# Layer 1 attention of a two-layer network: other tiles, other masks, another order of the same sums

## The reference

```python
Q, K, V = x @ wq, x @ wk, x @ wv                  # 16 heads of 8
# a token sees, in its own block of 32 and the one ahead of it, the 32 last keys
base = (j > i) & (j <= i + W)
blk0 = (jnp.arange(nb) > 0)[:, None, None] | (j >= W)[None, :, :]
sc = jnp.einsum('bhnid,bhnjd->bhnij', Qb, Kw) / np.sqrt(D)
p = jax.nn.softmax(jnp.where(mask, sc, -jnp.inf)); local = p @ Vw
# 64 latents, each the mean of 8 tokens; token s sees latents up to s // 8
GQ = x @ wgq; GK = pool(x @ wgk); GV = pool(x @ wgv)
lmask = jnp.arange(N_LATENTS)[None, :] <= (jnp.arange(Sx) // chunk)[:, None]
rem = softmax(where(lmask, GQ GK^T / sqrt(8), -inf)) @ GV @ r_out_w
gl = sigmoid(einsum('bhsd,hd->bhs', Q, gate_local_w)); gr = sigmoid(... gate_remote_w)
out = (gl * local + gr * rem) @ w_out
```

## Time and profile before

| | us |
|---|---|
| median of 3 runs | 823.16 (821.97 to 823.99) |
| the profiled execution | 828.99 |
| its span, first to last instruction | 826.9 |
| mean granted TensorE clock, share of 2.4 GHz | 0.904 |
| layer 1 attention, from its first matmul to the end of its last addition | 259.6 to 618.6 |

### The profile page before, as it was taken

One profiled execution on the slowest core, in us unless ns is written; L12 is line 12 of the kernel. 1 busy time (PEld: TensorE's weight loads), 2 busy tenths in 40 slices (PEclk: granted clock), 3 DMA queues, 4 the chain that ended last, 5 costly groups with the idle time before them and its releaser, 6 DMA issues.

```text
span 826.9 us, 15605 instructions
## 1 busy us (share of the span) xinstructions
PE 654.0 (79%) x4213; PEld 542.3 (66%) x4217; DVE 448.2 (54%) x1243; ACT 375.0 (45%) x874; POOL 245.3 (30%) x292
## 2 busy tenths in 40 slices
PE   3859457763174799999999999999978899998950
PEld 3837346763073677777777787878757788887850
DVE  7488637751667867676776776676731111111116
ACT  2217414441023364646555555555314555555534
POOL 6065716656002222222222220000001343433430
PEclk9999669995555999999999999999967999999985
DMA  9992133341230000000000000000004444444539
GB/s 242 256 186 56 45 103 116 110 125 49 76 128 0 21 20 21 19 22 17 20 21 21 18 20 1 1 1 1 1 4 146 164 158 154 164 154 152 168 104 276
DMA packets 80840, 69.46 MB, mean 84 GB/s; under 512 B 8436, under 2 KB 66419, under 8 KB 80782
## 3 DMA queue, kind: packets, MB, share of 16 engines
q1 hardware_dynamic: 71616, 54.97, 23.9%
q0 software_dynamic: 6624, 12.70, 4.8%
q10 hardware_dynamic: 2542, 1.08, 0.5%
HBM read 22.63 MB, written 23.22 MB: 55 GB/s over the span
## 4 chain that ended last, share of the span: by engine, by line
PE 40%; issue 19%; SPq 19%; DVE 11%; DMA 6%; POOL 3%; ACT 1%; DVEq 1%; POOLq 0%; ACTq 0%; another core or an unknown queue 0%
PE psum L1424 9%; PE psum L1386 5%; PE psum L1405 5%; SPq L1097 5%; PE psum L1395 4%; SPq L1110 4%; PE psum L1432 3%; SPq L1120 3%; SPq L242 3%; DMA ydram<-arena,g_id 3%; PE psum L1371 3%; POOL ydram L819 2%; DMA arena<-ydram 2%; PE psum L1359 2%; PE psum L1380 2%
## 5 line engine op out<-in xcount | busy, mean ns | idle before, releaser
L678 POOL DMA_INDIRECT sorted<-xr_all,slot x96 | 94.7, 987 | 190.2 <-DVE arena L1654 162.7
L1209 POOL DMA_INDIRECT ydram<-arena,f_id x71 | 68.7, 967 | 241.4 <-DVE f_id L1185 220.5
L1550 ACT ACTIVATE arena<-arena 128x512 f32<-128x512 f32 x96 | 60.5, 630 | 133.9 <-DVE arena L1654 133.8
L1170 ACT ACTIVATE arena<-psum,b1T 128x128 f32<-128x128 f32 x284 | 81.2, 369 | 78.8 <-PE psum L1139 68.8
L1651 DVE TENSOR_REDUCE arena<-psum 128x8 f32<-128x512 f32 x96 | 66.4, 691 | 66.8 <-PE psum L1386 34.8
L1193 DVE TENSOR_TENSOR arena<-psum,b_bc 128x128 f32<-128x128 f32 x71 | 20.7, 292 | 145.5 <-PE psum L1150 74.8
L1424 PE MATMUL psum<-arena 128*128 128x66 f32 (+1 forms) x768 | 97.6, 267 | 0.1
L1424 PEld LDWEIGHTS psum<-arena 128*128 128x128 f32 x768 | 95.7, 196 | 0.3 <-ACTq L1556 0.3
L1139 PE MATMUL psum<-arena 128*128 128x128 f32 x568 | 82.4, 290 | 16.3 <-DMA arena<-arena 12.7
L1139 PEld LDWEIGHTS psum<-arena 128*128 128x128 f32 x568 | 71.3, 197 | 28.6 <-issue 21.6
L1150 PE MATMUL psum<-w,arena 128*128 x568 | 80.6, 285 | 0.4
(11 more groups left out here) (267 smaller groups left out, 1086.9 us busy)
## 6 DMA issues: line engine op xcount, KB each, us to landing
arena<-arena SPq DMA_DIRECT2D x71, 256.0 KB
arena<-ydram SPq DMA_DIRECT2D x24, 256.0 KB, 4.0
arena<-mix SPq DMA_DIRECT2D x40, 128.0 KB
sorted<-pre_row SPq DMA_DIRECT2D x1, 4680.0 KB
arena<-sorted SPq DMA_DIRECT2D x71, 65.0 KB
sorted<-pre_row SPq DMA_DIRECT2D x1, 2600.0 KB, 21.6
arena<-sorted SPq DMA_DIRECT2D x10, 260.0 KB, 3.1
x_all<-in_L_attn_x_dram SPq DMA_DIRECT2D x8, 256.0 KB, 5.4
```

The costliest lines, as they stand in the source:

```text
L678: g.indirect_dma_start(out=dst, out_offset=bass.IndirectOffsetOnAxis(ap=slot[:, choice, t:t + 1], axis=0), in_=xr_all[:, t, :], in_offset= ...
L1170: ins = act.activation(f_hT[rr % 4][:, j * P:(j + 1) * P], psum[:, 2 + rr % 2, j * P:(j + 1) * P], ACT.Relu, bias=b1T[:, bass.ds(e * FC + ...
L1209: g.indirect_dma_start(out=ydram, out_offset=bass.IndirectOffsetOnAxis(ap=f_id[rr][:, :], axis=0), in_=f_y[rr], in_offset=None, bounds_che ...
L1550: act.activation(c_p[s % 3], c_sx[s % 2], ACT.Exp).then_inc(c_pr, 1)
```

## The change

The whole attention of layer 1 is written anew; what it computes is the same.

- The window scores lie with 128 tokens on the partitions. Each block of 32 tokens and each group of 4 heads is a matmul of its own, of a 32x32 part of the array (32 channels of the group, 32 tokens) against 256 columns (4 heads x 64 key places); 64 of them a batch in place of 16, and no bf16 mask matmuls but four of 128 columns for the first block. Keys are masked by the head (`head_m`) and kept once per head; the queries are plain.
- Since a token sees exactly 32 of its 64 key places, DVE lays the two blocks over each other (`copy_predicated` by `later`), and maximum, subtraction, exponential and transposes work on 4 x 4 x 32 places. After the transposes `split` multiplies by `m_prev` and `m_cur` into two parts.
- `values` is, for each tile of 128 tokens, 32 matmuls of 32 weight columns against 36 columns (4 heads x 8 channels and the denominator), 128 a batch; `pick` and the mask by group go. The values and the gates are projected with tokens as the weights: 64 matmuls of 32 against 32 columns, and 16 for both gates.
- Latent scores, exponentials, transposes and products of tile t cover only the first 16 (t + 1) latents.
- The sum of window and latents is formed with tokens on the partitions, and transposed once (`cbT`).
- Four PSUM banks hold window scores of 256 tokens at a time, and all else passes a ring of the four others in the order of the lists `even` and `odd`.
- PE waits, before its first projection, for the routing to have read PSUM (`s_rt`), and the zeroing by GpSimd (`attn1_init`) moves to before the norm of layer 1. The scatters wait for a third as many softmaxes.
- Set-up: other masks, and tables padded with zeros; one more small load.

```diff
+            def scores(u):
+                b, s = u // 2, u % 2
...
+                emptied(pe, "Q", b)
+                emptied(pe, "K", b)
+                if u:
+                    pe.wait_ge(c_sxr, 2 * u)
+                for tt in range(2):
+                    for k in range(G):
+                        n = (2 * s + tt) * G + k
+                        for g in range(G):
+                            row = slice(W * g, W * g + W)
+                            mm = pe.matmul(psum[W * k:W * k + W, g, tt * 256:(tt + 1) * 256],
+                                           c_q[b % 2][row, n * W:(n + 1) * W], c_kz[b % 2][row, :, n * W:n * W + W2],
+                                           start=True, stop=(n > 0), skip_group_check=True)
...
+            def values(b, s):
...
+                    for g in range(G):
+                        for c, part in enumerate((c_pp, c_pc)):
+                            for k in range(G):
+                                n = t * G + k
+                                at_ = tt * G * HE + g * HE
+                                pe.matmul(o[W * k:W * k + W, at_:at_ + HE],
+                                          part[t % 2][:, g * P + k * W:g * P + (k + 1) * W],
+                                          c_v[b % 2][:, n + c, g, :, :].rearrange("p h e -> p (h e)"),
+                                          start=(c == 0), stop=(c == 1), skip_group_check=True)
...
+                if name == "V":
+                    for n in range(NB):
+                        for h in range(G):
+                            mm = pe.matmul(o[W * h:W * h + W, n * W:(n + 1) * W], xnT(b, n * W, (n + 1) * W),
+                                           wv_h[:, h, :, :], start=True, stop=True, skip_group_check=True)
...
+            for b in range(B):
+                latent_scores(b, 0)
+                latent_scores(b, 1)
+                transposes(b, 0)
+                transposes(b, 1)
+                remote("remT", b - 1)
+                scores(2 * b + 1)
+                latent_transposes(b, 0)
+                latent_transposes(b, 1)
+                remote("remo", b - 1)
+                values(b, 0)
+                project("Q", b + 1)
+                project("K", b + 1)
+                latent_scores(b, 2)
+                latent_scores(b, 3)
+                transposes(b, 2)
+                transposes(b, 3)
+                scores(2 * b + 2)
+                remote("cbT", b - 1)
...
+            def window_softmax(u):
...
+                    ch.link(v.copy_predicated(cur, later[:, :].bitcast(I32).unsqueeze(1).unsqueeze(1)
+                                              .to_broadcast([P, G, G, W]), sv[:, :, :, 0, :]))
+                    mx = c_mx.rearrange("p (g h) -> p g h", g=G)
+                    ch.link(v.tensor_reduce(mx, cur, AX, ALU.max))
...
+            def split(b, t):
+                o, free = filled(v, f"T{t}", b)
+                ov = o.rearrange("p (g q) -> p g q", g=G)
+                for part, m in ((c_pp, m_prev), (c_pc, m_cur)):
...
             pe.wait_ge(c_init, 1)
-            attn1(pe, attn1_pe)
+            pe.wait_ge(s_l1, 1)
+            pe.wait_ge(s_rt, 6)
+            attn1_pe(pe)
```

More of the change, by code:

```diff
@@ L1263, in build @@
[L1263 to L1273 removed]
+        c_p = [view(512) for _ in range(2)]
@@ new lines, in build, with ring_uses @@
+        c_q = [mix0[:, k * S:(k + 1) * S] for k in range(2)]
+        c_xp8 = cmp_[:, 0:NL * LH]
+        c_cb, c_cbT = mix0[:, 2 * S:3 * S], mix0[:, 3 * S:4 * S]
+        wv_h = wv1[:, :].rearrange("p (g h e) -> p h g e", g=G, h=G)
+        first = ["Q", "K", "V", "G", "GX", "GQ"]
+        even = ["L0", "L1", "T0", "T1", "-remT", "LT0", "LT1", "-remo", "O0", "+Q", "+K"]
+        odd = ["L2", "L3", "T2", "T3", "-cbT", "LT2", "LT3", "O1", "-out", "+V", "+G", "+GX", "+GQ"]
+        def ring_uses():
+            seq = [(n, 0) for n in first]
@@ new lines, in ring_uses, with slot_of @@
+            seq += [(n, B - 1) for n in ("remT", "remo", "cbT", "out")]
+            return {use: k for k, use in enumerate(seq)}
+        uses_of = ring_uses()
+        r_rdy = [sem(f"r_rdy{n}") for n in range(4)]
+        r_free = [sem(f"r_free{n}") for n in range(4)]
+        (c_init, c_xpr, c_sr, c_sxr, c_pr, c_lpr, c_cbr) = (
+            sem(n) for n in "c_init c_xpr c_sr c_sxr c_pr c_lpr c_cbr".split())
+        def slot_of(name, b):
+            k = uses_of[name, b]
+            return psum[:, 4 + k % 4, :], r_rdy[k % 4], r_free[k % 4], k // 4 + 1
@@ L1427, in local_out @@
-            def local_out(hf):
-                pe.wait_ge(c_zr, batch(cur) * 8 + (4 * hf + 4))
-                o, rdy = begin(acc(f"loc{hf}", cur))
-                for j in range(HB):
-                    mm = pe.matmul(o[:, order[j] * W:(order[j] + 1) * W], c_z[hf][:, j, :, :].rearrange("p g c -> p (g c)"),
-                                   pick[:, :], start=True, stop=True)
-                mm.then_inc(rdy, 1)
-            def tail(name):
-                if not prev:
+                b, s = u // 2, u % 2
@@ new lines, in scores, with transposes, latent_scores @@
+                mm.then_inc(c_sr, 1)
+            def transposes(b, t):
+                pe.wait_ge(c_pr, b * T + t + 1)
+                o, rdy = begin(f"T{t}", b)
+                for g in range(G):
+                    mm = pe.transpose(o[:, g * P:(g + 1) * P], c_p[t % 2][:, g * P:(g + 1) * P], ident[:, :])
+                mm.then_inc(rdy, 1)
+            def latent_scores(b, t):
+                emptied(pe, "GQ", b)
+                emptied(pe, "GX", b)
+                o, rdy = begin(f"L{t}", b)
+                n = (t + 1) * P
+                pe.matmul(o[:, 0:n], c_gq[b % 2][:, t * P:(t + 1) * P],
+                          c_gk[b % 2].rearrange("p n h -> p (n h)")[:, 0:n], start=True, stop=True).then_inc(rdy, 1)
@@ new lines, in attn1_pe @@
+            scores(0)
+            for b in range(B):
[17 more added lines that the diff above has]
+                remote("cbT", b - 1)
+                latent_transposes(b, 2)
+                latent_transposes(b, 3)
+                values(b, 1)
+                remote("out", b - 1)
+                for name in ("V", "G", "GX", "GQ"):
+                    project(name, b + 1)
@@ new lines, in attn1_dve @@
+            pooled(0)
+            latent_operands(0)
+            window_softmax(0)
+            for b in range(B):
+                latent_softmax(b, 0)
+                latent_softmax(b, 1)
+                split(b, 0)
+                split(b, 1)
+                joined(b - 1)
+                window_softmax(2 * b + 1)
+                normalise(b, 0)
+                pooled(b + 1)
+                latent_softmax(b, 2)
+                latent_softmax(b, 3)
+                split(b, 2)
+                split(b, 3)
+                window_softmax(2 * b + 2)
+                normalise(b, 1)
+                onto_stream(b - 1)
+                latent_operands(b + 1)
```

713 lines of the change are left out of this document (321 added, 392 removed).

## The result

The changed kernel takes 737.2 us (four runs, 734.8 to 741.6) against 822.6 for the kernel before on the same chip: a ratio of 0.897, 95% interval 0.892 to 0.902. The forecast was 837, its range began at 750: wrong in sign and outside the range. The profiled run had 738.1 us with a span of 736.4.

The account below looks back on a forecast made before the run. TensorE was taken to bound each batch: 13.8 + 13.9 + 0.2 + 13.5 = 41.4 us, with 3 us of waits 44.4 against 42.38. Eight batches and the ends gave +13.4 us, 837 us; range 750 to 945.

Parts of the forecast that it names:

- Kept-price products: TensorE work keeping its old unit prices (Q, K, GQ, latents, transposes, GX, `remo`, `out`): 13.8 us a batch.
- (a): The 64 window score products on TensorE: one stream of 0.217 us each, 13.9 us a batch.
- (b): The 208 small value, V and gate products on TensorE: 0.065 us each, 13.5 us a batch.
- VectorE, 24.2 us: VectorE's work a batch, some 26 us with gaps; `copy_predicated` might add 2.8; not expected to bound.
- the first rival: Array parts all work side by side: 774 us, or 730 with VectorE's chain setting a batch near 31; chance 0.27.
- Waits, 3 us: TensorE's waits for PSUM banks a batch: 1.2 for the ring's bank, 1.1 at tile 3's transposes, 0.8 at first latent score.
- The clock rival: TensorE's clock falls to half under narrow matmuls: 1168 us for all the stage, 1000 for half; chance 0.10.
- The ends: Stage start and finish: first projection waits until 265.1, first scores end at 282.5, last batch ends in 8.5 us.
- The drains: Ten changes a batch between full-size work and parts empty TensorE: 0.16 us each, 1.6 a batch, 13 in all; kept within range.
- The scatters at nothing: GpSimd's scatters lose their spacing in the attention stage but cost nothing; a few us if their cover went.
- the floor: Each small TensorE record costs 0.06 us whatever its size: 208 x 0.053 = 11 us a batch more, 925 us; chance 0.08.
- no overlap at all: Window score products on TensorE do not overlap: 27.8 us a batch, 942 us for the kernel; chance 0.12.

Follow-up runs that it names:

- e3: Changed kernel with all 64 window score products a batch on one 32x32 part of the array (results differ): 1114.1 us.
- e12: Changed kernel with window scores from four row groups into one column group, eight records in a row on one part (results differ): 901.2 us.
- e14: Changed kernel with all 64 products of V in one column group instead of four in turn (results differ): 802.8 us.
- e5: Changed kernel with the shorter latents undone, so every tile handles all 128 latents: 745.3 us, ratio 0.905 to the kernel before.
- e10: Changed kernel with all 64 GpSimd scatters held until after the stage's last window softmax: six batches 186.8 us against 188.3.
- e9: Changed kernel with both score products of a part consecutive, four records in a row, next part in another row group: 786.2 us.
- e2: Changed kernel with window scores from one row group into four column groups, eight records in a row on one part (results differ): 930.6 us.
- e1: Changed kernel with window scores from four row groups into one column group, two records in a row on one part (results differ): 761.4 us.
- e8: Changed kernel with window scores from one row group, consecutive products going to another of four column groups (results differ): 832.1 us.
- v1: Changed kernel with next batch's products ordered GX, GQ, V, gates, and first batch's scores and softmax moved earlier: 714.7 us, ratio 0.868 to the kernel before.
- e6: Changed kernel without the masked copy that merges the key places (results differ): 720.8 us, ratio 0.875 to the kernel before.

## Why the prediction was wrong

- *Kept-price products, 13.8 us a batch*: right as far as it can be read; PE's busy 22.7 less the small ones (3.0 scores, 2.6 values, 2.2 V and gates) leaves 14.9.
- *(a), the scores: the step that failed first.* "the second record cannot start before the first has streamed its columns, and nothing behind it can either": the first half is right (0.216 apart on one part, e3), the second is wrong. Later products for other parts pass a waiting record. A record costs (1.49 - 0.37) / 63 = 0.018 us and not 0.108, so the 64 products cost 3.0 and not 13.9. I had the Trainium skill's rule as a rival, "TensorE: Matmul & The Clock Gate", section on packing small matmuls (sixteen parts 10.6 times as fast); the trace gives 13.8 / 1.49 = 9.3 times. The same section says that matmuls start and end strictly in program order; e12 speaks against it for records of one part in a row: in strict order at most one record in eight could overlap the one before, 57 x 0.216 = 12.3 us, and it took 8.16.
- *(b), the small products: the second term mis-sized.* The line through 0.11 and 0.06 gave 0.0325 a record, and in series that is what they cost (0.032, e14). What it left out is that four column groups overlap: (1.31 - 0.20) / 127 = 0.009. 416 records a batch cost 3.6 us and not 13.5. (a) and (b) together are 20.8 us of PE a batch too much, and 41.4 - 20.8 = 20.6, for 22.7 measured, of which 0.9 are the drains below.
- *VectorE, 24.2 us*: right, 23.3 busy; `copy_predicated` at 0.69 us, a lower bound of the range I gave. With PE at 22.7, this chain and its crossings set the batch, as the first rival said with "near 31" and 730 us; 31.4 us on average and 737 were measured. This rival had 0.27 and stood at the edge of my range, which cut off its lower end. What spoke for it, other parts, weights and banks for consecutive products, was better evidence than a rule of mine that no row bore out.
- *Waits, 3 us*: another kind came. The 1.2 for the ring's bank is there (PE waits for line 1659, 13.3 us in the stage), but the chain pays 6.1 a batch for crossings to PE.
- *The clock rival* came in part: the stage's granted clock was 0.86 on average. The two full-clock batches say 29.55 for 188.3 / 6 = 31.4: 11 us over six batches. By what it is set off stays open: e5 with more work on PE had full clock where the changed kernel had 0.80, e10 shows that the scatters don't do it, and e3 had 0.5 for long with one part working all the time.
- *The ends*: PE began at 264.0 (265.1 forecast), the first scores ended at 280.4 (282.5), and the end, from the last `remT` on, was 8.2 us (8.5). Right.
- *The drains*: they are there, 0.09 us each and 0.9 a batch, where 1.6 was reckoned and nothing put into the sum. A row had one already: in the earlier trace rows the record with 64 weight columns starts 0.06 us before the end of the one ahead (401.98 against 401.08 + 0.96), the others 0.16 or 0.17. *The scatters at nothing*: right here (188.3 with them, 186.8 without, e10) by luck, since the order of e9 makes it wrong by 36 us (217.3 - 181.0), and a single run of records in e10 by 84.
- *Slips of the sums*, which change nothing: 4.2 / 64 is 0.065 a product and so 0.033 a record, and the floor's 0.053 is 0.12 - 0.065 = 0.055. The price for no overlap at all, 942 us, left out the clock: e3, which has that for the scores, took 1114.1.

## What to carry to other kernels

Price small tiled matmuls as overlapping, give one part no more than two records in a row (four took 2.3 us where two took 1.5), and look for "issue" pauses inside one line's run where GpSimd issues indirect DMAs: holding these back gave 36 us in e9, and nothing to speak of in the changed kernel (1.5 us over six batches). When a change makes TensorE this cheap, forecast the batch from the next engine's busy time plus each crossing between engines, and put the work that the next engine waits for ahead of the work that nobody waits for (22 us here; of the 16.6 in six batches half came with the clock).

## What the hardware showed that I had not expected

- Going from full-size records to parts, or back, costs TensorE 0.09 us each time (the next record starts 0.07 us before the end of the one ahead, for 0.16 without a change).
- TensorE lets records for free parts pass waiting ones, and sharing rows costs nothing (e2 and e12 have the same starts; 3.66 us for e1 and e8).
- 128 records of 36 columns in 1.31 us: ten nanoseconds each, weight load included.
- While GpSimd issues scatters, runs of such records can stop again and again for multiples of 0.70 us: a 1.3 us run took 7.7 (e9) and 85 (e10). In the changed kernel the same run beside six scatters took 1.8.
- The clock was at half for most of the stage in e3 and e2 (mean 0.64 and 0.70), although PE was busy nearly all the time on one part or four. Over six batches it was 1.00 in e5, 0.96 in v1, 0.95 in e6 and 0.89 in the changed kernel: PE's busy share (0.84, 0.83, 0.82, 0.82) does not tell them apart.
